# Projection pieces of 512 columns in place of 256 in the second half of two attentions

## The chip, the cores and the metric

The kernel runs on one core of a Trainium2 chip. The metric is the device time of one execution in microseconds, and lower is better. The engines are named as the profile names them: PE is the matrix engine (PEld are its weight loads), ACT, DVE and POOL are the three elementwise engines, SP issues DMAs. PE writes its results into PSUM, which has eight banks of 128 partitions by 512 fp32 words; ACT and DVE read them from there.

## What is computed

The input x has 4 batches of 512 rows of 256 values. Four conditioned layers follow each other: a transformer layer with attention (layer 0), a state space layer (layer 1), a transformer layer with rotary attention (layer 2) and a low-rank adapter (layer 3). The change touches the two attentions alone. That of layer 2 reads:

```python
q = (xn @ Wq).reshape(B, N, H, D).transpose(0, 2, 1, 3)
k = (xn @ Wk).reshape(B, N, H, D).transpose(0, 2, 1, 3)
v = (xn @ Wv).reshape(B, N, H, D).transpose(0, 2, 1, 3)
cos, sin = rope_cos_sin(N, D)
q = q * cos + rotate_half(q) * sin
k = k * cos + rotate_half(k) * sin
attn = jnp.einsum('bhnd,bhmd->bhnm', q, k) * scale
attn = jax.nn.softmax(attn, axis=-1)
out = jnp.einsum('bhnm,bhmd->bhnd', attn, v)
```

xn is the normalised and modulated x; there are 16 heads of 16 values. Layer 0 has the same attention with biases on q, k and v and without the rotation.

## The kernel before

Both attentions are objects of one class `Attention` (`att0`, `att1`). The four batches of an attention run as one loop of 256 steps, n = 0 to 255, 64 to a batch and 16 to a group of four heads (`Attention.pe`). One step computes, for one head and one block of 128 keys:

- a score matmul of 512 columns (L683, "ST") into one of the three shared banks 7, 0 and 1; ACT turns it into exponentials in SBUF (L779);
- a second score matmul (L694) for a later head, 32 steps ahead, from which only the row maximum is wanted. These go to banks 2 to 5, and DVE reduces two of them at a time (L875).

The two matmuls of a step use 50 and 48 rows of the array, the one in its lower half and the other in its upper half, and run side by side; the text calls them a **pair**. After every fourth step come the four matmuls of exponentials by values (L715, "PV", bank 6). The stretch from one PV to the next, with four pairs, is called a **quad** below. A group of 16 steps has four quads: the **M quad** (steps 0 to 3 of 16), in which PE also transposes the maxima (L656, "M", read by DVE); the **O quad** (4 to 7), in which ACT also copies the finished output of a group from bank 6 (L736, "O"); the **third** (8 to 11) and the **fourth** (12 to 15).

Everything else that the attention needs is put in between by a table: `attention_schedule` gives each task a step number, and each engine runs, at each step, the tasks of that step that concern it, before the step's own pair. "Q", "K" and "V" are the pieces of the three projections, "RQ" and "RK" the rotation matmuls (L651, second attention only), "T" the transposes of a new batch, "PJ" the output projection. Batches 2 and 3 (b >= 2) use split operands: each product is three fp32r matmuls (high by high, high by low, low by high), so a piece of 256 columns has two halves of the contraction by three, six matmuls (L621 for Q and K, L629 for V). There are eight such Q and K pieces for a batch (two tensors, two halves of the heads, two halves of the columns) and four V pieces. They are put at every fourth step, at step 2 of a quad, hence after the second pair and ahead of the third: Q and K of batch 2 at steps 34, 38, ... 62, V of batch 2 at 74 to 86, Q and K of batch 3 at 98 to 126, V of batch 3 at 146 to 158. A quad with such a piece is called a quad with a piece, one with neither a piece nor another task of that size an **empty** quad.

Pieces, M, T, R and PJ use the same three shared banks as the scores. `slots` deals them out in turn, in the order of the steps, and `open` makes PE wait until the task three places earlier has been read:

```python
where = early if n < LEAD else SHARED if n <= TAIL else (7, 6)
add(key, where[turn % len(where)])
turn += 1
```

Q and K pieces are read out of PSUM by ACT (L755 with a bias, L758 without); V pieces by DVE in the first attention (L821, with a bias) and by ACT in the second (L762). POOL splits the results (task S), and DMAs carry them through DRAM into the layout that the score matmuls read (W, FILL), which are put 14 steps and more after the piece.

## Time and profile before

| | |
|---|---|
| median of 3 runs | 934.22 us (931.71, 934.22, 936.51) |
| the profiled execution | 934.88 us, its span 932.9 us |
| PE, DVE, ACT, POOL busy | 95%, 63%, 56%, 50% of the span |
| chain that ended last | PE 79%, DVE 9%, ACT 4%, issue 4%, POOL 3% |

The span runs from the first to the last instruction; the 2.0 us beside it lie around it. Of the rows below, those of the stage table give a stretch, its length, then for PE, PEld, DVE, ACT and POOL the busy time and the number of records, then PE's granted clock as a share of 2.4 GHz, the busy share of the DMA engines and their GB/s. The eight stretches of the second group run from one PV start to another, and hold every quad with a piece of batches 2 and 3: four of eight quads with Q and K, four of four quads with V. Those of the timeline give start, length, engine, line, operands and count, and in brackets the idle time before it and who ended it. PE records overlap, since its matmuls are pipelined: the pace of PE is read from the distance between starts.

### The profile page before, as it was taken

The numbers are of one execution on the slowest core, as the hardware profiler recorded it, in microseconds if no ns is written. First come the engines' busy times: TensorE is split into PE (matmuls) and PEld (weight loads), VectorE is DVE, ScalarE is ACT, GpSimd is POOL, SyncE is SP. The second block draws the span as 40 slices with busy tenths as digits, with TensorE's granted clock in tenths as the row PEclk, the third lists the DMA queues.
The fourth block names the chain that finished last, engine by engine and source line by source line (L and its number), as shares of the span: only waits on it lengthen the run. The fifth ranks groups of instructions, "written<-read, shape, count | busy, mean of one in ns | idle before, by whom it ended". The sixth has DMA issues, their size and how long they took to land.

```text
span 932.9 us, 14877 instructions
## 1 busy us (share of the span) xinstructions
PE 888.0 (95%) x5358; PEld 541.1 (58%) x5358; DVE 589.3 (63%) x928; ACT 521.2 (56%) x955; POOL 469.7 (50%) x626
## 2 busy tenths in 40 slices
PE   5999999999999999999999999999999999999997
PEld 3554444443347779677787774344444333687874
DVE  4687887888885465554533287778778895234323
ACT  2226878777775534444464531677867777744331
POOL 4393565655748636446544326658264116664330
PEclk7979999999999999999999999999999999999999
DMA  7565684666213030132223136545545531100001
GB/s 229 149 164 162 164 236 124 179 193 179 73 47 91 1 133 1 47 102 97 97 76 132 14 99 185 176 105 186 165 120 184 147 91 54 37 14 1 23 23 46
DMA packets 67088, 101.32 MB, mean 109 GB/s; under 512 B 19644, under 2 KB 30984, under 8 KB 66632
## 3 DMA queue, kind: packets, MB, share of 16 engines
q1 hardware_dynamic: 58584, 86.90, 31.4%
q0 software_dynamic: 5920, 10.90, 4.6%
q10 hardware_dynamic: 2512, 2.58, 1.0%
q8 instruction: 43, 0.70, 0.3%
q14 instruction: 29, 0.24, 0.1%
HBM read 64.65 MB, written 35.02 MB: 107 GB/s over the span
## 4 chain that ended last, share of the span: by engine, by line
PE 79%; DVE 9%; ACT 4%; issue 4%; POOL 3%; DMA 1%; ACTq 0%; DVEq 0%; POOLq 0%
PE PS L715 13%; PE PS L683 13%; PE PS L1141 12%; PE PS L1123 12%; PE PS L638 5%; PE PS L694 4%; PE PS L621 3%; DVE U L875 3%; PE PS L616 3%; PE PS L454 2%; ACT PH L779 2%; PE PS L651 2%; PE PS L629 1%; PE PS L1259 1%; PE PS L1247 1%
## 5 line engine op out<-in xcount | busy, mean ns | idle before, releaser
L875 DVE TENSOR_REDUCE U<-PS 128x2 f32<-128x1024 f32 x256 | 308.1, 1220 | 60.3 <-PE PS L694 59.0
L779 ACT ACTIVATE PH<-PS 128x512 f32<-128x512 f32 x512 | 277.1, 598 | 94.3 <-PE PS L683 91.3
L683 PE MATMUL PS<-UR 50*128 50x512 f32 x512 | 197.0, 454 | 9.3 <-ACT PH L779 4.7
L694 PE MATMUL PS<-UR 48*128 48x512 f32 x512 | 192.5, 471 | 5.9 <-DVE U L875 5.2
L1189 POOL TENSOR_TENSOR PHR<-PH,PHR 128x512 fp32r<-128x512 f32 x96 | 123.5, 1290 | 117.3 <-ACT PHR L1179 117.3
L683 PEld LDWEIGHTS PS<-UR 50*128 50x128 f32 x512 | 82.6, 186 | 151.2 <-ACT PH L779 84.4
L1141 PE MATMUL PS<-UR,PHR 128*128 128x256 f32 x768 | 158.6, 290 | 2.7 <-POOL PHR L1189 2.5
L715 PE MATMUL PS<-PH,U 128*32 128x512 f32 x1024 | 137.5, 610 | 0.0
L1141 PEld LDWEIGHTS PS<-UR,PHR 128*128 128x128 f32 x768 | 124.6, 189 | 20.1 <-issue 16.0
L1141 PE MATMUL PS<-W2R,PHR 128*128 128x256 f32 x384 | 108.2, 282 | 0.0
L1178 ACT ACTIVATE PH<-PS,col 128x512 f32<-128x512 f32 x64 | 43.9, 687 | 91.8 <-PE PS L1123 91.8
L694 PEld LDWEIGHTS PS<-UR 48*128 48x128 f32 x512 | 77.4, 187 | 23.9 <-DVE U L875 12.2
L1123 PE MATMUL PS<-UR 128*128 128x512 f32 x192 | 77.9, 406 | 2.3 <-DVE XNR L1213 1.9
L1123 PE MATMUL PS<-UR,W1R 128*128 128x512 f32 x192 | 76.1, 396 | 0.0
L1123 PE MATMUL PS<-XNR,UR 128*128 128x512 f32 x192 | 75.8, 395 | 0.0
L1141 PEld LDWEIGHTS PS<-W2R,PHR 128*128 128x128 f32 x384 | 72.2, 188 | 3.0 <-issue 1.2
L940 POOL TENSOR_TENSOR x<-x,tsc 128x256 f32<-128x256 f32 x32 | 23.5, 735 | 61.5 <-DVE tsc L848 60.9
L1178 ACT ACTIVATE PH<-PS 128x512 f32<-128x512 f32 x32 | 19.1, 597 | 53.2 <-PE PS L1123 53.2
L414 POOL TENSOR_TENSOR rs<-ve,mhalf 128x4 f32<-128x4 f32 x24 | 25.8, 1074 | 41.3 <-DVE ve L409 40.9
L929 POOL TENSOR_TENSOR U<-U 128x512 f32<-128x512 f32 x16 | 21.0, 1312 | 48.9 <-issue 30.8
L1825 ACT ACTIVATE xnorm<-x,rs 128x256 f32<-128x256 f32 x64 | 33.2, 591 | 20.9 <-POOL rs L448 20.9
L1179 ACT ACTIVATE PHR<-PS,col 128x512 fp32r<-128x512 f32 x64 | 43.7, 683 | 0.0
(256 smaller groups left out, 1387.5 us busy)
## 6 DMA issues: line engine op xcount, KB each, us to landing
UR<-d_parts SPq DMA_DIRECT2D x112, 192.0 KB, 4.2
d_parts<-UR SPq DMA_DIRECT2D x42, 256.0 KB
d_parts<-UR POOLq DMA_DIRECT2D x40, 256.0 KB, 5.4
d_o<-U SPq DMA_DIRECT2D x32, 256.0 KB, 2.5
U<-in_L_cond_W_dram SPq DMA_DIRECT2D x8, 1024.0 KB, 7.5
W<-in_L_cond_W_dram SPq DMA_DIRECT2D x24, 256.0 KB, 3.3
U<-d_o SPq DMA_DIRECT2D x32, 128.0 KB
U<-d_rec SPq DMA_DIRECT2D x16, 256.0 KB
```

The lines of the kernel that those rows point to most:

```text
L638: ins = pe.matmul(dst[:, 0:D], src[:, k, i * P:(i + 1) * P], w[:, k, :], start=(k == 0), stop=(k == 1))
L683: self.close(pe.matmul(dst, KP[g // 2][r:r + SROWS + 2, j, kt * P:(kt + 1) * P], QP[g // 2][r:r + SROWS + 2, j, :], start=True, stop=True) ...
L694: ins = pe.matmul(bank(2 + (w + 2) % 4), QP[g // 2][r:r + SROWS, j, qt * P:(qt + 1) * P], KP[g // 2][r:r + SROWS, j, :], start=True, stop= ...
L715: ins = pe.matmul(PS[32 * j:32 * j + 32, 6, :], Vt[b % 2][:, kt, 4 * g + j, :], PH[:, m % 2, j, :], start=(kt == 0), stop=(kt == 3))
L779: nc.scalar.activation(PH[:, m % 2, j, :], self.where("ST", n), ACT.Exp).then_inc(self.a_free, 1)
L875: v.tensor_reduce(mx[:, G % 2, :].rearrange("p (r c) -> p r c", r=2)[:, :, c // 2], PS[:, 2 + (w + 1) % 4:4 + (w + 1) % 4, :], AX.X, ALU.m ...
L1123: ins = pe.matmul(bank(4 + q % 2), w[:, k, c], a[:, b % 2, k, :], start=(k == 0 and i == 0), stop=(k == 1 and i == 2))
L1141: ins = pe.matmul(self.acc(b, t), a[:, q % 4, c], w[:, m, :], start=(m == 0 and i == 0 and t % 2 == 0), stop=(m == FM - 1 and i == 2 and s ...
L1178: nc.scalar.activation(PH[:, 0, q % 4, :], bank(4 + q % 2), self.func, bias=bias)
L1179: nc.scalar.activation(HH[:, q % 4, :], bank(4 + q % 2), self.func, bias=bias).then_inc(self.h_free, 1)
L1189: pool.tensor_tensor(PHR[:, 0, q % 4, :], PH[:, 0, q % 4, :], HH[:, q % 4, :].bitcast(F32), ALU.subtract).then_inc(self.h_low, 1)
L1825: ins = nc.scalar.activation(xnorm[:, t, :], x[:, TT * b + t, :], ACT.Identity, bias=rs[:, 3, t:t + 1], scale=rs[:, 2, t:t + 1])
```

## The change

In batches 2 and 3 of both attentions two neighbouring pieces become one, which fills a bank of 512 words. For Q and K its six matmuls have 512 columns where there were twelve of 256. For V, where the columns of x are the weights, twelve matmuls of 256 columns remain, six into each half of one bank. Of the table's entries only every second stays, at the later of the two steps; eight pieces of 256 columns become four, and four V pieces two. One instruction reads each piece out, of 512 columns. Batches 0 and 1 are as before.

```diff
                     at = -80 + 5 * q + part if first else -30 + 4 * (2 * q + part) if b == 1 else o - 30 + 4 * (2 * q + part)
-                    put(at, c, b, 2 * half + part)
+                    if b < 2 or part:
+                        put(at, c, b, 2 * half + part)
...
-            put(-18 + 4 * t if first else o + (18 if b == 3 else 10) + 4 * t, "V", b, t)
+            if b < 2 or t % 2:
+                put(-18 + 4 * t if first else o + (18 if b == 3 else 10) + 4 * t, "V", b, t)
...
-                                    ins = pe.matmul(dst[:, 0:D], wt[:, w, k, h], xt[:, k, c], start=(k == 0 and j == 0),
+                                    ins = pe.matmul(dst, wt[:, w, k, h], xt[:, k, :], start=(k == 0 and j == 0),
                                                     stop=(k == 1 and j == 2))
...
-                        for k in range(DH):
-                            for j, (xt, wt) in enumerate(((XNR[:, 0], WH), (XNR[:, 0], WAR), (XNR[:, 1], WH))):
-                                ins = pe.matmul(dst[:, 0:D], xt[:, k, i * P:(i + 1) * P], wt[:, 2, k, :],
-                                                start=(k == 0 and j == 0), stop=(k == 1 and j == 2))
+                        for t in range(2):
+                            c = slice((i - 1 + t) * P, (i + t) * P)
+                            for k in range(DH):
+                                for j, (xt, wt) in enumerate(((XNR[:, 0], WH), (XNR[:, 0], WAR), (XNR[:, 1], WH))):
+                                    ins = pe.matmul(dst[:, D * t:D * (t + 1)], xt[:, k, c], wt[:, 2, k, :],
+                                                    start=(t == 0 and k == 0 and j == 0), stop=(k == 1 and j == 2),
+                                                    skip_group_check=True)
...
-                        h, c = i // 2, slice(D * (i % 2), D * (i % 2 + 1))
+                        h, c = i // 2, slice(D * (i % 2), D * (i % 2 + 1)) if b < 2 else slice(0, T)
+                        src = src if b >= 2 else src[:, 0:D]
...
-                        v.tensor_tensor(Vt[b % 2][:, i, :, 0:HD],
-                                        self.where(kind, b, i)[:, 0:D].rearrange("p (h c) -> p h c", h=NH),
-                                        bias_bc[:, 0, :].rearrange("p (h c) -> p h c", h=NH),
+                        ts = slice(i, i + 1) if b < 2 else slice(i - 1, i + 1)
+                        n = ts.stop - ts.start
+                        v.tensor_tensor(Vt[b % 2][:, ts, :, 0:HD],
+                                        self.where(kind, b, i)[:, 0:D * n].rearrange("p (k h c) -> p k h c", h=NH, c=HD),
+                                        bias_bc[:, 0:1, :].rearrange("p k (h c) -> p k h c", h=NH).to_broadcast([P, n, NH, HD]),
                                         ALU.add).then_inc(self.m_free, 1)
```

In the changed kernel the lines of the loop stand some lines further down: L683 is L688, L694 is L699, L656 is L661, L715 is L720, L621 is L623, L779 is L787, L755 is L761, L736 is L741, L821 is L831, L875 is L885.

PE, first attention, the M quad of steps 32 to 35, in which the first Q piece of batch 2 stood. Before, from the second pair (the pairs are L683 and L694; XNR is the split x, W2R and WAR the split weights):

```order
L683 MATMUL PS<-UR 128x512
L694 MATMUL PS<-UR 128x512
L621 MATMUL PS<-XNR,W2R 128x256 x2
L621 MATMUL PS<-XNR,WAR 128x256
L621 MATMUL PS<-XNR,W2R 128x256 x2
L621 MATMUL PS<-XNR,WAR 128x256
L683 MATMUL PS<-UR 128x512
L694 MATMUL PS<-UR 128x512
L656 MATMUL PS<-ident,U 16x128
L683 MATMUL PS<-UR 128x512
L694 MATMUL PS<-UR 128x512
L715 MATMUL PS<-PH,U 32x512 x4
```

The same place after:

```order
L688 MATMUL PS<-UR 128x512
L699 MATMUL PS<-UR 128x512
L688 MATMUL PS<-UR 128x512
L699 MATMUL PS<-UR 128x512
L661 MATMUL PS<-ident,U 16x128
L688 MATMUL PS<-UR 128x512
L699 MATMUL PS<-UR 128x512
L720 MATMUL PS<-PH,U 32x512 x4
```

The M quad has lost its piece; in the O quad behind it the piece of six matmuls by 256 columns has become one of six by 512, in the same place between its second and third pair.

ACT, first attention, the stretch from the first Q piece of batch 2. Before (L779 are the exponentials, L736 is O, L755 reads Q with bq and K with col as the bias):

```order
L755 ACTIVATE U<-PS,bq 128x256
L779 ACTIVATE PH<-PS 128x512 x2
L736 ACTIVATE U<-PS 128x512
L779 ACTIVATE PH<-PS 128x512 x2
L755 ACTIVATE U<-PS,bq 128x256
L779 ACTIVATE PH<-PS 128x512 x4
L755 ACTIVATE U<-PS,col 128x256
L779 ACTIVATE PH<-PS 128x512 x4
L755 ACTIVATE U<-PS,col 128x256
L779 ACTIVATE PH<-PS 128x512 x4
```

After:

```order
L787 ACTIVATE PH<-PS 128x512 x8
L741 ACTIVATE U<-PS 128x512
L787 ACTIVATE PH<-PS 128x512 x2
L761 ACTIVATE U<-PS,bq 128x512
L787 ACTIVATE PH<-PS 128x512 x8
L761 ACTIVATE U<-PS,col 128x512
L787 ACTIVATE PH<-PS 128x512 x6
L741 ACTIVATE U<-PS 128x512
```

Each read of a piece stands where the second of two stood, two exponentials behind the start of its quad, and eight exponentials pass between two of them where there were four.

DVE, first attention, V of batch 3 (L875 the maxima, L821 the reads of V, L836 and L837 the reads of M, L841 a reciprocal of the softmax sums). Before:

```order
L821 TENSOR_TENSOR U<-PS,bias_bc 128x16x16
L836 TENSOR_SCALAR UR<-PS 16x128
L837 SCALAR_TENSOR_TENSOR UR<-PS,UR 16x128
L875 TENSOR_REDUCE U<-PS 128x2 x2
L821 TENSOR_TENSOR U<-PS,bias_bc 128x16x16
L875 TENSOR_REDUCE U<-PS 128x2 x2
L821 TENSOR_TENSOR U<-PS,bias_bc 128x16x16
L841 RECIPROCAL U<-U 128x32
L875 TENSOR_REDUCE U<-PS 128x2 x2
L821 TENSOR_TENSOR U<-PS,bias_bc 128x16x16
```

After:

```order
L846 TENSOR_SCALAR UR<-PS 16x128
L847 SCALAR_TENSOR_TENSOR UR<-PS,UR 16x128
L885 TENSOR_REDUCE U<-PS 128x2 x2
L831 TENSOR_TENSOR U<-PS,bias_bc 128x32x16
L885 TENSOR_REDUCE U<-PS 128x2 x2
L851 RECIPROCAL U<-U 128x32
L885 TENSOR_REDUCE U<-PS 128x2 x2
L831 TENSOR_TENSOR U<-PS,bias_bc 128x32x16
```

Two reads of twice the width are left of four, and the read of M no longer has a V read ahead of it in its quad.

## Rows read from the trace of the kernel before

**Rows 1.** The page: busy time of each engine, and the chain that ended last.

```profile
PE 888.0 (95%) x5358; PEld 541.1 (58%) x5358; DVE 589.3 (63%) x928; ACT 521.2 (56%) x955; POOL 469.7 (50%) x626
PE 79%; DVE 9%; ACT 4%; issue 4%; POOL 3%; DMA 1%; ACTq 0%; DVEq 0%; POOLq 0%
```

**Rows 2.** Stage table: stretch, length, busy PE, PEld, DVE, ACT, POOL, clock, DMA, GB/s.

```profile
91.83:118.60 26.77, 26.77 (x181) 12.71 (x179) 22.64 (x31) 21.97 (x44) 16.89 (x24) 1.00 0.63 180
144.85:171.60 26.75, 26.75 (x181) 12.71 (x179) 20.95 (x22) 21.96 (x43) 15.34 (x19) 1.00 0.55 144
610.58:640.79 30.21, 30.21 (x186) 13.77 (x185) 24.54 (x34) 21.84 (x44) 18.77 (x23) 1.00 0.48 132
667.55:697.75 30.20, 30.20 (x186) 13.75 (x185) 22.66 (x25) 21.85 (x44) 15.57 (x14) 1.00 0.48 128
124.40:137.97 13.57, 13.43 (x92) 6.35 (x90) 11.76 (x15) 9.32 (x19) 6.67 (x9) 1.00 0.88 242
185.62:199.18 13.56, 13.41 (x91) 6.34 (x89) 11.62 (x15) 9.28 (x18) 10.65 (x37) 1.00 0.53 149
647.27:660.67 13.40, 13.40 (x91) 6.37 (x90) 10.50 (x11) 10.83 (x23) 4.41 (x4) 1.00 0.63 206
712.68:726.03 13.35, 13.35 (x91) 6.34 (x90) 10.53 (x11) 10.80 (x22) 1.56 (x2) 1.00 0.45 123
```

**Rows 3.** Stage table, single quads: piece; empty; M, empty; RK and M; piece and RQ.

```profile
95.48:98.72 3.24, 3.24 (x25) 1.60 (x23) 2.63 (x3) 2.76 (x7) 0.00 (x0) 1.00 0.66 206
207.60:210.21 2.61, 2.54 (x18) 1.01 (x16) 2.36 (x3) 2.06 (x6) 1.27 (x1) 1.00 1.02 377
199.18:202.28 3.10, 2.67 (x19) 1.00 (x17) 2.65 (x4) 2.53 (x5) 1.54 (x8) 1.00 0.66 198
640.79:644.57 3.78, 3.56 (x21) 1.29 (x20) 2.88 (x3) 2.53 (x5) 3.62 (x4) 1.00 0.75 240
617.46:621.96 4.50, 4.50 (x26) 1.90 (x25) 3.11 (x4) 3.02 (x6) 0.00 (x0) 1.00 0.41 133
```

**Rows 4.** Timeline of a quad with a piece, from its piece.

```profile
97.14 0.51 PE L621 MATMUL PS<-XNR,W2R 128*128 128x256 f32 x2
98.05 0.50 PE L683 MATMUL PS<-UR 50*128 50x512 f32 x1
98.15 0.47 ACT L755 ACTIVATE U<-PS,bq 128x256 f32<-128x256 f32 x1
98.72 1.07 PE L715 MATMUL PS<-PH,U 128*32 128x512 f32 x8
99.71 0.50 PE L683 MATMUL PS<-UR 50*128 50x512 f32 x1
```

**Rows 5.** Timeline of an empty quad.

```profile
208.59 0.50 PE L683 MATMUL PS<-UR 50*128 50x512 f32 x1
209.13 1.58 ACT L779 ACTIVATE PH<-PS 128x512 f32<-128x512 f32 x3 [0.55 <-PE PS L683]
209.78 0.18 PEld L683 LDWEIGHTS PS<-UR 50*128 50x128 f32 x1 [0.39 <-ACT PH L779]
210.21 0.64 PE L715 MATMUL PS<-PH,U 128*32 128x512 f32 x4
```

**Rows 6.** The chain that ended last: twelve fp32r matmuls of 256 columns, six of 512.

```profile
336.96 1.41 PE PS L1141 x12
334.68 1.40 PE PS L1123 x6
```

**Rows 7.** Groups by line and shape: reads out of PSUM by ACT and DVE.

```profile
L755 ACT ACTIVATE U<-PS,bq 128x256 f32<-128x256 f32 x16 | 7.6, 475 | 19.5 <-PE PS L616 19.3
L1178 ACT ACTIVATE PH<-PS,col 128x512 f32<-128x512 f32 x64 | 43.9, 687 | 91.8 <-PE PS L1123 91.8
L821 DVE TENSOR_TENSOR U<-PS,bias_bc 128x256 f32<-128x256 f32 x16 | 6.7, 417 | 0.6 <-PE PS L638 0.4
L830 DVE TENSOR_TENSOR U<-PS,rope 128x512 f32<-128x512 f32 x16 | 11.1, 692 | 27.2 <-PE PS L651 27.2
```

More of the change, by code:

```diff
@@ L754, in task @@
                             bias = bq16[:, h:h + 1] if kind == "Q" else column("L0_bk", h)
-                            ins = nc.scalar.activation(o, src[:, 0:D], ACT.Identity, bias=bias,
+                            ins = nc.scalar.activation(o, src, ACT.Identity, bias=bias,
                                                        scale=1.0 / HD if kind == "Q" else 1.0)
                         else:
-                            ins = nc.scalar.activation(o, src[:, 0:D], ACT.Copy, scale=HD ** -0.5 if kind == "Q" else 1.0)
+                            ins = nc.scalar.activation(o, src, ACT.Copy, scale=HD ** -0.5 if kind == "Q" else 1.0)
                     elif kind == "V":
@@ L761, in task @@
                             act.wait_ge(self.pv_done, 16 * (b - 1))
-                        ins = nc.scalar.activation(Vt[b % 2][:, i, :, 0:HD],
-                                                   src[:, 0:D].rearrange("p (h c) -> p h c", h=NH), ACT.Copy)
+                        ts = slice(i, i + 1) if b < 2 else slice(i - 1, i + 1)
+                        ins = nc.scalar.activation(Vt[b % 2][:, ts, :, 0:HD],
+                                                   src[:, 0:D * (ts.stop - ts.start)].rearrange("p (k h c) -> p k h c", h=NH, c=HD),
+                                                   ACT.Copy)
                     ins.then_inc(self.a_free, 1)
@@ L820, in task @@
                             v.wait_ge(ld_bias, 96)
[L821 to L823 removed]
+                        ts = slice(i, i + 1) if b < 2 else slice(i - 1, i + 1)
+                        n = ts.stop - ts.start
+                        v.tensor_tensor(Vt[b % 2][:, ts, :, 0:HD],
+                                        self.where(kind, b, i)[:, 0:D * n].rearrange("p (k h c) -> p k h c", h=NH, c=HD),
+                                        bias_bc[:, 0:1, :].rearrange("p k (h c) -> p k h c", h=NH).to_broadcast([P, n, NH, HD]),
                                         ALU.add).then_inc(self.m_free, 1)
```

## The prediction

> **What bounds the kernel now.** I read the page first: PE is busy 95% of the span and carries 79% of the chain that ended last, while DVE, ACT and POOL stand at 63%, 56% and 50% [rows 1]. So the question is what PE's own time becomes, and whether PE begins to wait. An average does not answer it, so next comes the stage table for the stretches that hold the pieces [rows 2]. In the two stretches with the Q and K pieces of the first attention PE is busy 26.77 of 26.77 us and 26.75 of 26.75; in the second attention 30.21 of 30.21 and 30.20 of 30.20. V's four stretches show at most 0.15 us of idle PE in 13.57. The granted clock is 1.00 in all eight, the upper level of 2.4 GHz. All eight together last 167.81 us; nothing outside them is changed by the edit.
>
> Third, single quads [rows 3]. A quad with a piece takes 3.24 us, and PE is never idle in it. An empty quad takes 2.61. The difference, 0.63, is less than what the piece takes out of PE's time: from the piece's start at 97.14 to the next pair at 98.05 are 0.91 us [rows 4]. An empty quad at PE's own pace would thus take 3.24 - 0.91 = 2.33; it takes 2.61, so 0.28 of it is waiting. The timeline shows for what [rows 5]: the first pair starts at 208.59, ACT begins its exponential 0.54 later, and the fourth pair starts at 209.78, with its weight load idle for 0.39 until ACT. Four scores share three banks, so the fourth of a quad needs the first one's exponential to be done. A piece after the second pair fills just this gap. That is the whole problem: **a piece costs 0.63 us where its quad is otherwise empty, not 0.91**, and the change empties every second quad.
>
> **The change part by part.**
>
> *The merged quad.* Six matmuls of 512 columns take 1.40 us where they stream, twelve of 256 take 1.41 [rows 6]. So a Q or K pair of pieces costs the array the same, and V keeps its twelve matmuls as they were. A lone piece of six by 256 streams for 1.41 / 2 = 0.70 and takes 0.91, so each piece costs 0.21 for going in and out between the half-array pairs and full-array matmuls. The merged piece takes 1.40 + 0.21 = 1.61, and its quad 3.24 + 0.70 = 3.94. Each of the 24 merges (4 for Q and K and 2 for V, in 2 batches of 2 attentions) saves 0.21 of PE.
>
> On this place bears a rule of the Trainium skill ("TensorEngine Tiling (Array Packing)", Key Properties): changing the tiling mode of the array drains it. It speaks for the change, and by that rule the trace agrees, with the 0.21 above; taken alone it would give the whole 24 x 0.21 = 5 us, the first rival below.
>
> *The quad that loses its piece.* Its price is read from quads that already have none [rows 3]. In the third quad of a group: 2.61. In the M quad: 3.10, where PE is busy 2.67. In the second attention some of them keep a rotation matmul: RK and M together without a piece took 3.78; RQ alone without a piece does not occur. Its lower bound is the quad with piece and RQ less the piece, 4.50 - 0.91 = 3.59; its upper bound is the 3.78 of the quad that has M besides. I take the middle, 3.69; four such quads make this uncertain by 0.4 us either way.
>
> *The sum.* The merged pieces fall into O and fourth quads, the emptied ones are M and third quads.
> - Q and K, first attention, per batch: 2 x (3.10 + 3.94 + 2.61 + 3.94) = 27.18, against 26.77 and 26.75: +0.41, +0.43.
> - Q and K, second attention, per batch: M empty 3.10, RQ 3.69 twice, RK and M 3.78, and four merged of 3.94: 30.02, against 30.21 and 30.20: -0.19, -0.18.
> - V, per batch: 3.10 + 3.94 + 2.61 + 3.94 = 13.59, against 13.57, 13.56, 13.40, 13.35: +0.02, +0.03, +0.19, +0.24.
>
> The sum is **+0.95 us**. The profiled execution took 934.88 us, so it would take 935.8. That execution lies 0.66 above the median of 934.22; from the median the time is **935.2**.
>
> *Reads out of PSUM.* ACT reads 256 columns of Q in 475 ns; of 512 columns with a bias from a column the nearest row is 687 [rows 7]. That saves ACT 0.26 us per merge, off the path: ACT is busy 2.76 of 3.24 us even in a quad with a piece [rows 3], and where PE waits for it, it waits for the first exponential's latency and not for ACT's load. What could hurt is that one read gets longer. In the timeline the next pair starts at 98.05 when the piece is through, ACT starts to read the piece at 98.15 and is done at 98.62; with 687 ns, at 98.84. The piece's bank is next wanted by the first pair of the next quad, at 99.71 [rows 4]. So 0.87 us of cover is left, and I cost it at nothing. If the cover were gone, 0.21 per merge would be added. For V in the first attention DVE reads 256 in 417 ns, and 692 is its nearest row for 512 from PSUM [rows 7]. This pushes the following maximum back by 0.28, which can hold up the third pair of the next quad by some 0.1; that quad is an empty one whose fourth pair waits anyway. Nothing, at most 4 x 0.1.
>
> A rule of the skill speaks against larger reads ("Perfetto Trace Analysis", Optimizing Scalar/DVE Operations): where ACT and DVE are not saturated but cause bubbles elsewhere, smaller instructions may let work finish sooner. Here ACT is not saturated. If the rule held at this place, the sum would grow by the 24 x 0.21 of the second rival; by the row the bubble has other causes, and the 0.87 stand in between.
>
> *DVE in the emptied quads.* An empty quad holds 2.36 us of DVE in 2.61 [rows 3]. Batch 3's statistics fall into four quads of Q and K of batch 2: the stretches of batch 2 hold 22.64 and 24.54 us of DVE, those of batch 3 20.95 and 22.66 [rows 2], so 1.7 to 1.9 more. Some 0.4 of it in an empty third quad would make 2.8 of DVE in 2.61 of time. The merged quads on both sides leave DVE over 1 us free each, and it may lag by a pair of banks. I take nothing; the bound is 0.2 per attention for it.
>
> *Order and rotation.* Twelve tasks fewer are dealt out per attention. Twelve is a multiple of three and of two, so all banks behind the stretch are the same as before. POOL's splits come after a read that ends some 0.4 us later than now; the DMAs stand ten steps behind them, the transfers into the matmuls' layout later still. Nothing waits for that.
>
> **The rivals.**
>
> *The saved switches come through.* If the emptied quads ran at PE's own pace, for instance because ACT's exponentials start earlier once it is relieved, each merge would give its full 0.21: 24 x 0.21 = 5.0 us, and 929.2. Against it: in an empty quad ACT has nothing queued when the first pair arrives (idle 0.55 before its exponential [rows 5]), so relief cannot start it earlier. Half of this (931.7) would need waits that go away in half of the quads.
>
> *The longer read reaches the path (slower).* Place: the first pair after a merged piece, or the pair that wants its bank. Price: 0.687 - 0.475 = 0.21 per merge, 24 times, 5.1 us, and with the sum 935.2 + 5.1 = 940.3. It decides when the read ends over 0.87 us later than I work out, for instance if ACT took two exponentials first. Against it: ACT takes its tasks in order, and the read stands ahead of the third exponential.
>
> *It does not do what it says for Q and K,* in that one matmul of 512 columns costs other than two of 256. Rows 6 leave 0.01 us per piece for that: 16 x 0.01 = 0.2 us, no case of its own.
>
> **How the numbers follow.** A measurement of this kernel can tell about 0.5% from no change, 4.7 us (929.5 to 938.9). Chances: the sum as worked out, within 2 us of it, 0.78; a part of the saved switches comes through, 0.10, of which 0.06 end below 929.5; longer reads or DVE reach the path, 0.12, of which 0.06 end above 938.9. So faster 0.06, same 0.88, slower 0.06. The range: known bounds are -0.4 and +1.2 us (RQ 0.4 either way, DVE 0.4, V 0.4), the runs of before spread by 2.5 us below and 2.3 above their median, and half of each rival is taken in: 931.0 to 939.0.
>
> **What would show it right or wrong.** In the profile after: merged quads of 3.94 with no idle PE; third quads of 2.61 and M quads of 3.10 between them, their fourth pair waiting for ACT; RQ quads of 3.6 to 3.8; the eight stretches 168.8 us in all; ACT's read of a piece 0.69 and about 0.1 after the next pair begins. Wrong would be: third quads near 2.33 (first rival), a pair behind a merged quad that waits for ACT's or DVE's read (second rival), a merged quad other than 3.9 to 4.0, or a change outside the eight stretches.

## The result, and the profile after

The changed kernel takes **943.16 us** (median of 9 runs, 937.64 to 946.82) beside 935.86 for the kernel before (9 runs, 931.18 to 940.59): ratio **1.0086, interval 1.0059 to 1.0112**. It is slower by about 7 us, where 935.2 and no clear change had been forecast, and it lies above the range of 931 to 939. The profiled execution took 941.19 us.

The page of the kernel after: span, busy times, the granted clock in 40 slices (tenths of 2.4 GHz, 9 is 90% or more), the chain that ended last.

```profile
span 939.3 us, 14613 instructions
PE 886.5 (94%) x5262; PEld 535.7 (57%) x5262; DVE 585.9 (62%) x924; ACT 513.2 (55%) x935; POOL 468.9 (50%) x626
PEclk9989999999999999999999998699999999999999
PE 71%; DVE 8%; ACT 6%; POOL 5%; issue 4%; DMA 3%; SPq 1%; ACTq 0%; DVEq 0%; POOLq 0%
```

Against [rows 1] PE's busy time hardly moved: 886.5 us instead of 888.0. What is new stands in the clock's row: a slice of 8 and one of 6 in the second half, which is from 564 to 610 us.

The stage table after, the same eight stretches as [rows 2]: Q and K of the first attention, Q and K of the second, V of the first, V of the second (columns as there).

```profile
88.80:115.92 27.12, 25.83 (x157) 11.02 (x155) 22.23 (x31) 20.32 (x38) 17.40 (x25) 1.00 0.65 184
142.23:169.34 27.11, 25.82 (x156) 11.02 (x154) 20.51 (x22) 20.31 (x38) 15.13 (x18) 1.00 0.56 143
616.49:646.39 29.90, 28.82 (x162) 11.97 (x160) 24.55 (x34) 20.28 (x40) 19.27 (x23) 1.00 0.48 133
673.49:703.39 29.90, 28.81 (x162) 11.92 (x160) 22.55 (x25) 20.28 (x39) 16.24 (x14) 1.00 0.46 127
121.72:135.35 13.63, 13.04 (x92) 6.49 (x90) 11.58 (x13) 9.11 (x19) 6.08 (x8) 1.00 0.87 251
183.36:196.98 13.62, 12.97 (x92) 6.40 (x90) 11.54 (x13) 9.09 (x18) 10.71 (x37) 1.00 0.52 152
652.87:666.60 13.73, 13.14 (x91) 6.51 (x90) 10.31 (x11) 10.02 (x21) 4.11 (x4) 1.00 0.68 219
718.30:731.90 13.60, 12.94 (x91) 6.37 (x89) 10.29 (x11) 9.99 (x20) 1.56 (x2) 1.00 0.40 125
```

They add up to 168.61 us, 0.80 more than the 167.81 before; 0.95 had been forecast. PE is busy for 161.38 us in them instead of 167.52, so the saving is there, and it has turned into waits. The edited part of the program did what was forecast, and the other 6 us or so are somewhere else. Single quads of the kernel after, beside [rows 3]: merged Q or K piece; empty third quad; empty M quad; RQ alone; merged V piece.

```profile
98.45:102.36 3.91, 3.91 (x25) 1.80 (x23) 3.03 (x4) 2.63 (x5) 2.33 (x3) 1.00 0.46 142
95.83:98.45 2.62, 2.39 (x19) 0.91 (x17) 2.38 (x3) 2.19 (x6) 2.27 (x2) 1.00 0.37 103
102.36:105.46 3.10, 2.67 (x20) 0.99 (x18) 2.87 (x4) 2.67 (x6) 2.75 (x3) 1.00 0.70 182
623.52:627.19 3.67, 3.44 (x20) 1.21 (x18) 3.11 (x4) 2.59 (x6) 0.00 (x0) 1.00 0.50 149
655.48:659.43 3.95, 3.95 (x30) 2.24 (x29) 2.77 (x3) 2.63 (x7) 1.57 (x2) 1.00 0.70 249
```

The timeline of an empty quad and the merged one behind it, for the waits (beside [rows 4, 5]).

```profile
95.83 1.07 PE L720 MATMUL PS<-PH,U 128*32 128x512 f32 x8
...
98.01 0.50 PE L688 MATMUL PS<-UR 50*128 50x512 f32 x1 [0.23 <-ACT PH L787]
...
98.45 1.06 PE L720 MATMUL PS<-PH,U 128*32 128x512 f32 x8
...
100.11 0.73 PE L623 MATMUL PS<-XNR,W2R 128*128 128x512 f32 x2
...
101.69 0.50 PE L688 MATMUL PS<-UR 50*128 50x512 f32 x1
...
102.36 1.06 PE L720 MATMUL PS<-PH,U 128*32 128x512 f32 x8
```

The fourth pair of the empty quad waits for ACT; no pair of the merged quad waits for anything. The reads, grouped by line and shape (beside [rows 7]).

```profile
L761 ACT ACTIVATE U<-PS,bq 128x512 f32<-128x512 f32 x4 | 2.8, 688 | 2.6 <-PE PS L623 2.6
L831 DVE TENSOR_TENSOR U<-PS,bias_bc 128x512 f32<-128x512 f32 x4 | 2.8, 692 | 1.4 <-PE PS L633 1.4
```

**Where the time came from.** The softmax weights times V (PV, L715 before and L720 after) are in every quad of both attentions, so the first and the last of them frame the part of the program between the start and the last MLP. One row for each kernel: the first and the last start of this line's weight loads, before and then after.

```profile
L715 PEld LDWEIGHTS PS<-PH,U x1024: 106/109/150, 68.9 to 800.8; 128*32 128x32 f32 x171
```

```profile
L720 PEld LDWEIGHTS PS<-PH,U x1024: 105/109/152, 65.9 to 806.7; 128*32 128x32 f32 x171
```

From 731.9 us this part has grown to 740.8, by 8.9. (The start was 3.0 us shorter in this execution of after and the end 0.5 longer, which makes the 6.4 between the spans. The start lies ahead of the first changed instruction, and its length varies between executions of one and the same kernel: the first PV starts at 68.9 and at 70.5 us in two profiles of the kernel before.) Now this part is cut at two places where the program is the same in both kernels. First row: from the last PV of the first attention to the first PV of the second, which holds MLPs and the early tasks of the second attention, and not one changed instruction; call it the **gap**. Second row: the seven quads behind it; call them the **head**. Six of them are unchanged; the seventh is the M quad that opens the Q and K stretch of the second attention (it starts at 610.58 before and 616.49 after), so it is counted among the eight stretches too. Before:

```profile
274.19:588.16 313.97, 299.27 (x1754) 234.95 (x1752) 171.32 (x325) 145.06 (x249) 163.97 (x210) 1.00 0.27 85
588.16:614.22 26.06, 25.65 (x145) 10.77 (x144) 18.16 (x19) 18.89 (x36) 16.37 (x15) 0.93 0.49 150
```

After:

```profile
271.96:589.87 317.91, 303.94 (x1754) 237.82 (x1752) 171.09 (x325) 145.02 (x249) 164.49 (x211) 0.98 0.27 84
589.87:619.59 29.72, 28.89 (x139) 11.30 (x138) 17.62 (x17) 18.43 (x35) 14.97 (x14) 0.78 0.42 120
```

The gap has grown by 3.94 us and the head by 3.66. In the gap the same 1754 matmul records are busy for 303.94 us instead of 299.27, while DVE and ACT are where they were, and the clock's column falls from 1.00 to 0.98; in the head it falls from 0.93 to 0.78. The head's seventh quad has lost its piece and takes 3.10 us instead of 3.64. The six unchanged quads alone, before and after:

```profile
588.16:610.58 22.42, 22.01 (x123) 9.09 (x122) 15.28 (x15) 15.90 (x31) 12.88 (x12) 0.92 0.47 147
589.87:616.49 26.62, 26.22 (x122) 10.31 (x122) 14.96 (x14) 15.89 (x31) 12.03 (x11) 0.76 0.40 115
```

They have grown by 4.20 us. So of the 8.9 us, 0.80 is the edited stretches, 3.94 the gap and 4.20 the six quads, which is all of it. PE's busy time fell by 6.1 us in the edited stretches and rose by 4.7 and 4.2 in these two places, with the same matmuls; that is the main reason why its total hardly moved (the shorter start took some off again).

Inside the gap, PE's timeline at the border of two MLP layers. Before:

```profile
449.34 0.47 PE L1123 MATMUL PS<-UR 128*128 128x512 f32 x1 [1.22 <-DVE XNR L1213]
...
450.94 0.50 PE L1123 MATMUL PS<-UR 128*128 128x512 f32 x1 [0.68 <-DVE XNR L1213]
451.28 0.39 PE L1123 MATMUL PS<-XNR,UR 128*128 128x512 f32 x1
...
452.19 1.03 PE L1259 MATMUL PS<-U 128*128 128x256 f32 x4
```

After:

```profile
447.02 0.47 PE L1133 MATMUL PS<-UR 128*128 128x512 f32 x1 [1.21 <-DVE XNR L1223]
...
448.62 0.50 PE L1133 MATMUL PS<-UR 128*128 128x512 f32 x1 [0.67 <-DVE XNR L1223]
448.96 0.52 PE L1133 MATMUL PS<-XNR,UR 128*128 128x512 f32 x1
449.28 0.63 PE L1133 MATMUL PS<-UR,W1R 128*128 128x512 f32 x1
...
450.56 1.91 PE L1269 MATMUL PS<-U 128*128 128x256 f32 x4
```

The same two idle stretches of PE stand in both, 1.2 and 0.7 us long, behind the same chain of DVE instructions. Before, four matmuls behind them take 1.03 us; after, the same four take 1.91. The windows of the kernel after show what differs: the granted clock is 0.50 right behind (1.2 GHz), and on average 0.52 in a longer piece around the head. Such a stretch at 0.50 is called a **fall** below (a "dip" in the recorded expectations).

```profile
449.50:452.50 3.00, 3.00 (x11) 2.53 (x11) 1.56 (x10) 1.26 (x2) 0.98 (x4) 0.50 0.01 3
585.00:602.00 17.00, 17.00 (x53) 6.68 (x53) 8.87 (x10) 7.18 (x15) 13.53 (x12) 0.52 0.38 124
```

A further fall begins at 568 us, behind an idle of 0.82. Each of the two in the gap lasts about 3.4 us, in which 1.7 us of work is left undone: 2 x 1.7 = 3.4 of the 3.94. The long one, 585 to 602, reaches from the gap's end into the head, where the kernel before has one of 3.4 us. Ahead of it stand three idle stretches of 0.20, 0.49 and 0.29 us, and PE is busy throughout it.

### The profile page after: what moved, and what is told of

It reads as the page before. It is cut to its first block, busy times and chain, and to the rows that moved or that the text cites. A ratio compares the mean times of both kernels' runs of the same rounds, so it can differ in the third digit from the quotient of the medians.

```text
span 939.3 us, 14613 instructions
## 1 busy us (share of the span) xinstructions
PE 886.5 (94%) x5262; PEld 535.7 (57%) x5262; DVE 585.9 (62%) x924; ACT 513.2 (55%) x935; POOL 468.9 (50%) x626
## 4 chain that ended last, share of the span: by engine, by line
PE 71%; DVE 8%; ACT 6%; POOL 5%; issue 4%; DMA 3%; SPq 1%; ACTq 0%; DVEq 0%; POOLq 0%
PE PS L720 12%; PE PS L1151 12%; PE PS L688 11%; PE PS L1133 11%; PE PS L643 5%; ACT PH L787 4%; PE PS L699 3%; PE PS L623 2%; PE PS L618 2%; PE PS L456 2%; DVE U L885 2%; PE PS L656 1%; DMA d_parts<-UR 1%; PE PS L633 1%; PE PS L1269 1%
## 5 line engine op out<-in xcount | busy, mean ns | idle before, releaser
L885 DVE TENSOR_REDUCE U<-PS 128x2 f32<-128x1024 f32 x256 | 307.5, 1219 | 69.3 <-PE PS L699 68.4
L787 ACT ACTIVATE PH<-PS 128x512 f32<-128x512 f32 x512 | 274.4, 599 | 94.5 <-PE PS L688 92.0
L688 PE MATMUL PS<-UR 50*128 50x512 f32 x512 | 195.0, 457 | 11.9 <-ACT PH L787 8.8
L699 PE MATMUL PS<-UR 48*128 48x512 f32 x512 | 189.8, 469 | 7.7 <-DVE U L885 5.9
L688 PEld LDWEIGHTS PS<-UR 50*128 50x128 f32 x512 | 83.6, 189 | 160.6 <-ACT PH L787 91.5
L720 PE MATMUL PS<-PH,U 128*32 128x512 f32 x1024 | 139.1, 616 | 0.0
L699 PEld LDWEIGHTS PS<-UR 48*128 48x128 f32 x512 | 77.9, 188 | 26.0 <-DVE U L885 12.7
```

What stands on the lines that cost most here:

```text
L688: self.close(pe.matmul(dst, KP[g // 2][r:r + SROWS + 2, j, kt * P:(kt + 1) * P], QP[g // 2][r:r + SROWS + 2, j, :], start=True, stop=True) ...
L699: ins = pe.matmul(bank(2 + (w + 2) % 4), QP[g // 2][r:r + SROWS, j, qt * P:(qt + 1) * P], KP[g // 2][r:r + SROWS, j, :], start=True, stop= ...
L720: ins = pe.matmul(PS[32 * j:32 * j + 32, 6, :], Vt[b % 2][:, kt, 4 * g + j, :], PH[:, m % 2, j, :], start=(kt == 0), stop=(kt == 3))
L787: nc.scalar.activation(PH[:, m % 2, j, :], self.where("ST", n), ACT.Exp).then_inc(self.a_free, 1)
L885: v.tensor_reduce(mx[:, G % 2, :].rearrange("p (r c) -> p r c", r=2)[:, :, c // 2], PS[:, 2 + (w + 1) % 4:4 + (w + 1) % 4, :], AX.X, ALU.m ...
```

## The experiments

Two theories stand against each other from the second group of experiments on. **Place** (P): the change moves all that follows by 0.8 us, and where the work stands decides behind which idle of PE the clock falls. Then any shift of the same size does the same, in the kernel before too. **Merged kernel** (M): something that the merged form itself does (other intervals of ACT and DVE, waits of PE in the stretches) lowers the clock or costs time; then a shift without it does nothing, and the merged kernel stays slow wherever it stands. The first four expectations name two earlier theories: A, by which the falls come where they come, in either kernel, and B, by which the changed kernel brings them about.

The profiles of all of them first; the texts behind say what follows. A **pad** of 2, 4 or 6 is that many extra matmuls ahead of the gap, a **fill** is extra matmuls where PE is idle. "Profiled" is the time of the execution that the columns behind the ratio are read from. "First to last PV" is read as above. "To the gap" is the distance from the PV that opens the first stretch of [rows 2] (at 91.83 us in the kernel before) to the start of the gap; where it differs, the work behind comes earlier or later by as much. "Low clock" gives the start of falls between 75 us and the last 10 us of the span, with their length (3.4 us where none is given). The ratio is to the kernel before, on the same chip.

| kernel | median us | profiled | ratio, 95% | first to last PV | to the gap | gap | head | low clock at |
|---|---|---|---|---|---|---|---|---|
| before | 935.86 | 934.88 |  | 731.9 | 182.4 | 313.97 | 26.06 | 588 |
| before again | 934.94 | 934.79 | 1.0006, 0.9976 to 1.0037 | 730.2 | 182.2 | 313.99 | 24.47 | none |
| after | 943.16 | 941.19 | 1.0086, 1.0059 to 1.0112 | 740.8 | 183.2 | 317.91 | 29.72 | 449, 568, 585 (17) |
| after again | 942.19 | 938.40 | 1.0057, 1.0026 to 1.0089 | 736.2 | 183.1 | 317.28 | 25.52 | 451, 570, 591 |
| Q and K only | 938.94 | 939.01 | 1.0043, 1.0021 to 1.0065 | 735.4 | 183.1 | 317.25 | 25.52 | 453, 572, 593 |
| V only | 937.43 | 932.44 | 1.0018, 0.9987 to 1.0050 | 731.9 | 182.4 | 313.96 | 26.06 | 585 |
| before, pad 2 | 943.52 | 944.25 | 1.0063, 1.0028 to 1.0099 | 740.7 | 183.2 | 318.28 | 28.47 | 452, 571, 588 (13.7), 780 |
| before, pad 4 | 937.58 | 938.14 | 1.0023, 0.9995 to 1.0050 | 734.7 | 184.0 | 315.51 | 25.86 | 571 |
| before, pad 6 | 940.76 | 946.17 | 1.0068, 1.0030 to 1.0107 | 744.5 | 187.2 | 318.25 | 28.49 | 246 (6.8), 454, 574, 591 (13.6) |
| after, pad 4 | 937.95 | 945.85 | 1.0042, 1.0001 to 1.0083 | 742.8 | 184.9 | 316.68 | 27.90 | 571, 588 (13.6), 779 (10.2) |
| after, fill 1 | 939.37 | 941.46 | 1.0022, 0.9987 to 1.0058 | 738.3 | 183.1 | 314.89 | 28.02 | 585 (13.7), 776 (6.8) |
| after, fill 1 and 2 | 935.68 | 935.45 | 0.9985, 0.9961 to 1.0010 | 734.1 | 183.2 | 314.53 | 25.49 | 589 |
| before, fill 1 and 2 | 938.65 | 940.26 | 1.0029, 1.0005 to 1.0054 | 736.5 | 182.4 | 314.52 | 26.05 | 589, 774 (10.2) |
| before, pad 2, fill 1 and 2 | 935.07 | 934.86 | 0.9973, 0.9949 to 0.9996 | 732.0 | 183.2 | 314.49 | 24.51 | none |

One profile is one execution, and executions of a kernel differ in their falls: the kernel before has one at 588 us in its first profile and none in the second. So a profile shows where the clock can fall, and the median over the runs how often it does. Some profiles are far from the median: that of V only is the fastest of its runs, and those of pad 6 and of the changed kernel with pad 4 are at the slow end of theirs. Where Q and K are merged, the head's seventh quad is 0.54 us shorter, whatever the clock does.

All 28 falls of the last column begin 0.2 to 1.6 us behind the end of an idle stretch of PE, and they stand at five places of the program: at about 450 us (idle of 1.2 and 0.7 us), 570 (0.8), 585 to 593 (0.2 to 0.5, two or three times), 774 to 780 (0.5 and 0.4) and 246 (0.5 and 0.4).

### The two kernels again

No edit, twelve runs of each beside the kernel before.

> The kernel before, unchanged, for a second profile of it and more pairs of time and clock. The profile after shows the eight stretches as forecast (168.7 us) and some 5 us lost at a place that the change does not touch: from 585 to 602 us, ahead of the first piece of the second attention's batch 2, PE ran at the lower clock. Theory A (the dip of the clock falls where it falls, in either kernel): this profile has dips at other places or of other length than the first one's, the ratio stays within 0.5% of 1, and some of its runs have a clock as low as those of after (0.972 to 0.982). Theory B (the changed kernel itself brings the dip about): the dip at 588 us is again short here, some 2 us, and the clock of the runs stays at 0.984 or above.

Measured: 934.94 us, ratio 1.0006 (0.9976 to 1.0037). Gap and head of its profile:

```profile
275.72:589.71 313.99, 299.49 (x1754) 234.90 (x1753) 171.21 (x325) 145.05 (x249) 163.81 (x210) 1.00 0.27 85
589.71:614.18 24.47, 24.07 (x145) 10.07 (x145) 18.16 (x19) 18.87 (x36) 16.35 (x15) 1.00 0.51 150
```

The gap is the same to 0.02 us. The head is 1.59 shorter, which is what its 3.4 us of low clock cost in the first profile.

> The changed kernel, unchanged, once more. Theory A: ratio to before anywhere between 1.001 and 1.009, and nearer to 1.001 where the clocks of the two come out alike; the dip of 17 us at 585 to 602 us is absent or shorter in this profile. Theory B: ratio 1.008 again, and PE again at the lower clock from about 585 to 602 us. Both: the eight stretches 168.7 us in all, within 0.3 us.

Measured: 942.19 us, ratio 1.0057 (1.0026 to 1.0089).

```profile
274.07:591.35 317.28, 302.65 (x1755) 237.12 (x1753) 170.73 (x325) 145.03 (x249) 163.77 (x210) 0.99 0.27 85
591.35:616.87 25.52, 24.68 (x139) 9.79 (x138) 17.96 (x18) 18.43 (x35) 15.80 (x15) 0.93 0.47 140
```

The slowdown is there again, and so are the two falls in the gap, although this execution reached the place 2.1 us later than the first. (The kernel before reached it 1.5 us later the second time, and had no fall there in either profile.) The long fall at the head is not; there is one of 3.4 us. Two falls cost 317.28 - 313.99 = 3.3 us. The eight edited stretches take 168.7 us again, as expected.

Neither A nor B holds as it was put. Against A, the gap's two falls come back in the kernel after and stay away in the one before. Against B, the kernel before has runs at a mean clock of 0.972 and 0.977, and the kernel after has a profile without the long fall.

### One half of the change at a time

Only Q and K merged; the V part of the change is undone:

```diff
         for t in range(TT):
-            if b < 2 or t % 2:
-                put(-18 + 4 * t if first else o + (18 if b == 3 else 10) + 4 * t, "V", b, t)
+            put(-18 + 4 * t if first else o + (18 if b == 3 else 10) + 4 * t, "V", b, t)
```

> Only Q and K pieces are merged; V's four pieces of 256 columns stay. Worked out from the quads, the stretches of Q and K cost +0.47 us together and V's nothing. Theory A: ratio 1.0005 with the rest from the clock. Theory B, where the shift of one attention's work against the rest makes the dip: ratio near 1.008 if Q and K are what shifts it, near 1.0005 if V is.

Measured: 938.94 us, ratio 1.0043 (1.0021 to 1.0065). Its gap:

```profile
275.69:592.94 317.25, 302.60 (x1755) 237.13 (x1753) 170.73 (x325) 145.04 (x249) 163.72 (x210) 0.99 0.27 85
```

Only V merged; the Q and K part is undone:

```diff
-                    if b < 2 or part:
-                        put(at, c, b, 2 * half + part)
+                    put(at, c, b, 2 * half + part)
```

> Only V pieces are merged; Q and K stay at 256 columns. Worked out from the quads +0.48 us. Theory A: ratio 1.0005 with the rest from the clock. Theory B: near 1.008 if V's merging brings the dip about, near 1.0005 otherwise.

Measured: 937.43 us, ratio 1.0018 (0.9987 to 1.0050). Its gap:

```profile
271.32:585.28 313.96, 299.55 (x1754) 234.93 (x1752) 171.22 (x325) 145.19 (x249) 163.96 (x210) 1.00 0.27 85
```

In the first attention Q and K move all that follows by 0.35 + 0.36 = 0.71 us and V by 0.06 + 0.06 = 0.12 (stretches after against [rows 2]). The kernel with 0.71 has both falls in the gap, the one with 0.12 has neither ("to the gap": 183.1 and 182.4). That is as P has it, but M could still say that the merged Q and K do it. The ratio of Q and K only, 1.0043, is clear of the 1.0005 that A gave it and only half of the 1.008 of B; that of V only can't be told from 1.0005, and its profile is one execution, the fastest of twelve.

### A shift without the change

This tells the two apart. The kernel before gets nothing but extra matmuls of 256 columns in fp32, in front of the last output projection of batch 0 in the first attention, at about 184 us. By the length of the same matmuls beside them, two cost 0.86 us, four 1.7 and six 2.6; "to the gap" grows by 0.8 with two and by 1.6 with four. Their result is overwritten by the matmuls behind.

```diff
                         src, w = (XN[:, b % 2], WA[:, 2]) if kind == "V" else (yT, WA[:, 3])
+                        if self.a == 0 and (kind, b, i) == ("PJ", 0, 3):
+                            for _ in range(2):
+                                pe.matmul(dst[:, 0:D], src[:, 0, i * P:(i + 1) * P], w[:, 0, :], start=True, stop=True)
```

> The kernel before, with two extra fp32 matmuls of 256 columns (0.43 us each, of which the result is overwritten) ahead of the last output projection piece of the first attention, at about 182 us. It shifts all that follows by 0.86 us, as merging Q and K does (0.8), and merges nothing. Theory P (place): after the merges the clock falls at the pair of PE idles at 446 to 449 us and again at 570 us, since the same work comes 0.8 us later; so here the gap from the last PV of the first attention to the first PV of the second grows from 314.0 to 317.3 us, with the clock low behind the two idles, and the ratio is 1.004 to 1.007. Theory M (the merged kernel itself, by its quads of uneven activity or its shorter program): the gap stays 314.0 and the ratio is 1.001.

Measured: 943.52 us, ratio 1.0063 (1.0028 to 1.0099). Gap and head:

```profile
275.43:593.71 318.28, 304.38 (x1754) 237.88 (x1753) 171.16 (x325) 145.04 (x249) 164.77 (x211) 0.98 0.27 85
593.71:622.18 28.47, 28.07 (x145) 11.25 (x145) 17.87 (x18) 18.88 (x36) 15.25 (x14) 0.84 0.42 128
```

**0.86 us of matmuls, put into the kernel before, give the slowdown of the changed kernel**: its gap (318.28 and 317.91 us), a long fall at the head, and a time that is 6 us higher by the ratio and 8 by the medians. Nothing is merged in it. Theory M is not needed, and P has made the prediction that M could not.

The same with four:

```diff
-                            for _ in range(2):
+                            for _ in range(4):
```

> As before_pad2 with four extra matmuls, a shift of 1.7 us. Theory P: some other set of dips than at 0 and at 0.86 us, so a time that does not lie on a line with the pad. Theory M: gap 314.0, ratio 1.002.

Measured: 937.58 us, ratio 1.0023 (0.9995 to 1.0050), a gap of 315.51 with one fall. **Twice the extra work costs less than half as much**: the median is 6 us lower. A cost that grew with the work could not give that. The intervals of the two ratios overlap, but the two kernels ran beside each other on one chip, ten runs each, and their means differ by 4.8 us with a 95% interval of 2.3 to 7.4. The gaps of the profiles, 318.28 with two falls and 315.51 with one, say the same. (The head of this profile, 25.86 us at full clock, holds 1.24 us in which PE waits for a DMA; that is no matter of the clock.)

With six:

```diff
-                            for _ in range(2):
+                            for _ in range(6):
```

> As before_pad2 with six extra matmuls, a shift of 2.6 us. Theory P: the same gap and the same dips as the changed kernel with four extra ones, whose shift is 0.8 + 1.7 = 2.5. Theory M: gap 314.0, ratio 1.003.

Measured: 940.76 us, ratio 1.0068 (1.0030 to 1.0107). The mean is above that of four by 3.8 us (0.9 to 6.8), so the cost goes up, down and up again with the padding. Both falls in the gap are back, with a new one of 6.8 us at 246. That one stands ahead of the gap, so "to the gap" is 187.2, 4.8 us more than without padding and not 2.6.

And four in front of the same projection of the changed kernel, whose shift is then 0.8 + 1.7 = 2.5 us, about that of six in the kernel before:

```diff
                         src, w = (XN[:, b % 2], WA[:, 2]) if kind == "V" else (yT, WA[:, 3])
+                        if self.a == 0 and (kind, b, i) == ("PJ", 0, 3):
+                            for _ in range(4):
+                                pe.matmul(dst[:, 0:D], src[:, 0, i * P:(i + 1) * P], w[:, 0, :], start=True, stop=True)
```

> The changed kernel with four extra matmuls, 1.7 us more work. Theory P: gap as in before_pad6, and if that is 314.0 the time falls to that of the changed kernel or under it, in spite of the added work. Theory M: gap 317.3 as in the changed kernel, ratio 1.009 to 1.010.

Measured: 937.95 us, ratio 1.0042 (1.0001 to 1.0083). That it should show the falls of six in the kernel before is a miss: there is none near 450 us and none at 246. The two kernels do not reach the gap at the same place after all, since the fall at 246 moved the other one: 184.9 here, 187.2 there. So this comparison does not test P. Why six matmuls in the kernel before bring a fall at 246 us and this kernel has none is open. What holds is the other half: its median is 5.2 us under that of the changed kernel, with 1.7 us more to do. M, by which the merged kernel stays slow wherever it stands, is hard to keep. The intervals of the two ratios overlap, though (1.0001 to 1.0083 and 1.0059 to 1.0112), and the runs of this kernel lie far apart (932.34 to 946.37), so this alone doesn't end M; the fills below do.

The column "to the gap" sorts the ten profiles without fills, merged or not. At 182.2 to 182.4 us the gap holds neither fall (three profiles), at 183.1 to 183.2 both that at about 450 and that at 570 (four, one of them without any merge), at 184.0 and 184.9 only that at 570 (one kernel of each kind), at 187.2 both again. The time from the start of the span does not sort them: the gap starts at 274.19 us in the kernel before, without a fall, and at 274.07 in the second profile of the changed kernel, with two.

### Work in the idle of PE

If idle of PE is what the clock falls behind, work put there must take the falls away. Fill 1 puts five matmuls of 512 columns where PE waits 1.2 us for DVE, into a bank whose own first matmul overwrites them:

```diff
                 c = slice(m * P, (m + 1) * P)
+                if self.l == 1 and q == FM:
+                    for _ in range(5):
+                        pe.matmul(bank(4 + q % 2), W1R[:, 0, 0:P], W1R[:, 0, 0:512], start=True, stop=True)
```

> The changed kernel, with five extra matmuls of 512 columns (1.17 us, result overwritten) on PE where it sat idle for 1.21 us at 446 us, in the first product of the second batch of the layer 1 MLP. They add no time there. If the idle PE is what the clock fell for, the dip at 449 to 453 us is gone, the gap is shorter than 317.3 by some 1.7 us (which by itself moves the work behind it, so the later dips may change), and the ratio comes down from 1.006-1.009 to about 1.004. If the fall has nothing to do with the idle, it stays, and the ratio too.

Measured: 939.37 us, ratio 1.0022 (0.9987 to 1.0058). The gap is 314.89, and the falls at 449 and 568 are both gone. The long one at the head stays; it begins at 585, in the last 5 us of the gap.

Fill 2 adds ten more at the head, into bank 6 while it is free: three before the first wait for the maxima, and seven at the pairs that wait there. A wait makes sure that the last early piece has been read out of bank 6.

```diff
+                        for _ in range(3 if self.a and b == 0 else 0):
+                            pe.matmul(bank(6), QP[0][0:SROWS, 0, 0:P], KP[0][0:SROWS, 0, :], start=True, stop=True)
                         pe.wait_ge(self.sm_free, 8 * (b + 1))
...
                 if self.a:
                     pe.wait_ge(mlp1.h_free, FM * B)
+                    for t in [t for t in self.lead() if t in self.place and self.place[t][0] == 6][-1:]:
+                        self.wait_read(pe, *t)
...
+                        for _ in range({4: 2, 8: 1, 30: 1, 32: 2, 34: 1}.get(w, 0) if self.a else 0):
+                            pe.matmul(bank(6), QP[g // 2][r:r + SROWS, j, qt * P:(qt + 1) * P],
+                                      KP[g // 2][r:r + SROWS, j, :], start=True, stop=True)
                         if w % 2 == 0 and w >= 4:
                             pe.wait_ge(self.sm_free, w // 2 - 1)
```

> As after_fill1, and ten more extra matmuls of 512 columns into the unused bank 6 where PE waits for DVE's maxima at the head of the second attention (558 to 568 and 582 to 585 us). Idle there are some 2.6 us, and the extra ones stream for 2.3, of which I expect 0.5 to 1 us on the path. If idle is the cause: the dips at 568 and at 585 to 602 us are gone or short, the gap near 314, the clock near 0.99, and the ratio 1.001 to 1.003. If not: dips as before, ratio 1.009.

Measured: 935.68 us, ratio 0.9985 (0.9961 to 1.0010), lower than the 1.001 to 1.003 that were expected. The place at 449 us in this kernel:

```profile
448.07 1.30 PE L1138 MATMUL PS<-W1R 128*128 128x512 f32 x5
...
451.05 0.50 PE L1143 MATMUL PS<-UR 128*128 128x512 f32 x1 [0.72 <-DVE XNR L1233]
...
452.29 1.03 PE L1279 MATMUL PS<-U 128*128 128x256 f32 x4
```

The first idle is filled, the second is still there, and the four matmuls behind take 1.03 us again. **With fifteen matmuls more the changed kernel takes 7.5 us less and stands level with the kernel before.** The intervals of the ratios with and without the fills, 0.9961 to 1.0010 and 1.0059 to 1.0112, lie apart, and the second measurement of the changed kernel, 1.0026 to 1.0089, does too. With every merge in place the slowdown is gone, so it is no property of the merged form; M falls.

Both fills in the kernel before (the same edits; fill 1 is shown, that of fill 2 stands above):

```diff
+                if self.l == 1 and q == FM:
+                    for _ in range(5):
+                        pe.matmul(bank(4 + q % 2), W1R[:, 0, 0:P], W1R[:, 0, 0:512], start=True, stop=True)
```

> The kernel before with both fills. Its profiles had at most one dip of 3.4 us behind 582 us, worth 1 to 2 us in the head of the second attention. Theory P with idle as the cause: ratio 0.998 to 1.001. If the extra matmuls cost on the path what they stream: 1.003.

Measured: 938.65 us, ratio 1.0029 (1.0005 to 1.0054), a miss: they do not leave it as it was. The gap is 314.52, half a microsecond more, and the profile has a fall of 10.2 us at 774, far behind the fills. Taking away falls at two places is thus no remedy of its own. That the fills brought this one by their shift is not shown: other kernels have falls there too (780, 779 and 776 us).

And with two padding matmuls besides (only these are shown):

```diff
+                        if self.a == 0 and (kind, b, i) == ("PJ", 0, 3):
+                            for _ in range(2):
+                                pe.matmul(dst[:, 0:D], src[:, 0, i * P:(i + 1) * P], w[:, 0, :], start=True, stop=True)
```

> The kernel before with the pad of 0.86 us (ratio 1.006 by itself) and both fills. Theory P with idle as the cause: the fills take back the slowdown of a pad just as that of the merges: ratio 1.001 to 1.003, dips at 452, 571 and 588 gone or short. Otherwise 1.006 to 1.009.

Measured: 935.07 us, ratio 0.9973 (0.9949 to 0.9996), the lowest ratio of all and below the 1.001 to 1.003 that were expected.

```profile
275.03:589.52 314.49, 302.40 (x1769) 237.01 (x1767) 171.38 (x325) 145.18 (x249) 164.01 (x210) 1.00 0.27 85
589.52:614.03 24.51, 24.11 (x145) 10.10 (x144) 18.16 (x19) 18.89 (x36) 16.40 (x15) 1.00 0.50 148
```

No fall from 75 us to the last few microseconds, in a kernel that has some 4 us of matmuls more than the kernel before, and two padding matmuls more than the one that lost 0.3% just now. I would not hand this over as a better version: it is 0.3%, and by P the next edit moves it.

## Why the prediction was wrong

**What bounds the kernel: right.** PE does, and no stretch is lost to another engine.

**The merged quad, 3.94: right.** 3.91 to 3.96, with PE busy throughout, so the 0.21 for going in and out of the half-array pairs is paid once instead of twice.

**The quad that loses its piece: right.** Third quads 2.62 (forecast 2.61), M quads 3.10, with the fourth pair waiting 0.2 us for ACT (in M quads M waits as long besides). RQ alone, which had to be bounded between 3.59 and 3.78, took 3.67 (I took 3.69).

**The sum, +0.95: right.** +0.80 in the eight stretches, which take 168.5 to 168.7 us in every profile of a kernel with all merges. All of the 24 merges together saved PE's time and gave it back to the waits of the emptied quads, as worked out.

**Reads out of PSUM, nothing: right.** ACT's read takes 688 ns and DVE's 692, and no pair waits for either. The fear that larger reads bring bubbles did not come true here: the pair behind the merged piece starts with no idle.

**The rivals: neither came.** The emptied quads did not run at PE's pace, and the longer read did not reach the path. The slower rival's time of 940.3 is near the result, but by accident: its mechanism shows in no row.

**The step that failed** is the sentence in the part on what bounds the kernel, "nothing outside them is changed by the edit". As a statement on instructions it is true. As one on time it is false: 8.1 of the 8.9 us between first and last PV came from the gap and the six quads behind it, where no instruction changed. I had taken the granted clock of 1.00 in the eight stretches as a fixed property of the kernel, and left the clock out of the rest. The profile of before gave a hint that I passed over: its own head stood at 0.93, with a fall at 588 us behind short idle, so the clock was able to fall in the second half too. The runs gave another: before spreads from 931.18 to 940.59, and its runs lie along their clock (of 35 beside the first experiments, 931.21 us at a mean clock of 0.996, 942.02 at 0.978). With its median at 0.988 and that of after's runs at 0.980, those two give (942.02 - 931.21) / 0.018 = 6.0 us per 0.01, and 0.8 x 6.0 = 4.8 of the 7.3 us between the medians; another 0.8 is the edited stretches, and 1.7 are not accounted for in the medians. So the range was too narrow by a term it did not have: the effect of any shift on the falls of the clock, about -2.5 to +8 us by the ratios of the experiments (0.9973 to 1.0086), against -0.4 and +1.2 for all bounds that I had.

What stays open: behind which idle the clock falls is not worked out here. The changed kernel with fill 1 lost the fall at 568 us too, although the idle of 0.82 there was not filled; four padding matmuls took away the fall at 450 us and kept the one at 571. The fills also move what follows, so they don't prove alone that the filled idle was the cause; that the same idle stretches stand in the kernel before at full clock shows that idle is not enough by itself. That a shift of 0.8 us without any merge brings the same falls and the same slowdown is shown; by what rule the place decides is not.

## What to carry to other kernels

Where an edit shifts the work behind it, even by less than a microsecond, compare identical stretches of the two profiles by their granted clock before any story on the edited part; a ratio within about 1% can be the clock's alone. To learn what an edit is worth by itself, run it with a few padding matmuls ahead of the rest as well, at two or three sizes: a cost that doesn't grow with the padding is one of place. And when a forecast says "no change", its range must hold what the clock does to a kernel whose spread between runs is itself a matter of the clock.

## What the runs showed of the hardware

- The granted clock fell from 2.4 to 1.2 GHz (0.50 in the rows) right behind idle stretches of PE of 1.21 and 0.67 us, of 0.82 us, and of 0.2 to 0.5 us two or three times, with dense matmuls ahead of them and behind; in other kernels of this study it did not, behind the same idle. A fall lasted 3.4 us in 19 cases of 28 and 6.8 to 17 in the others, at PE busy throughout in the one of 17. The Trainium skill ("TensorE: Matmul & The Clock Gate", A second HAM failure mode: psum-queue depth-cycling) says that frequent short idle between groups of matmuls can make the clock go to and fro. The traces agree in part: the idle behind which it fell was short, but it was not frequent, two or three stretches ahead of most falls and a single one of 0.82 us ahead of that at 568. They add that a kernel can stand at the edge of it.
- 0.86 us of extra matmuls at 184 us raised the time by 6 us (ratio) to 8 us (medians), and 1.7 us of them by 2 to 3; work in PE's idle lowered that of the changed kernel by 7.5.
- Between the half-array pairs and full-array matmuls going in and out costs about 0.2 us of PE, whether a piece is long or short: from its start to the next pair a piece takes 0.91 us before, 0.21 more than the 0.70 it streams, and a merged one 1.58 to 1.62 us, 0.18 to 0.22 more than the 1.40.
